# A two-layer graph network on one core: node projection from a transposed copy of x, later zeros, and an output bias added in two parts

## The reference

```python
# layer 0: attention over heads, one gathered row per node
xt = (x @ weight).reshape(-1, 4, 64)
alpha = softmax(leaky_relu((xt[src] * attn_l).sum(-1) + (xt[dst] * attn_r).sum(-1), 0.01), axis=1)
tmp = einsum('nh,nhd->nd', alpha[:n], xt[dst[:n]])
x = layernorm(x + tile(tmp over 4 heads))
# layer 1: messages over the 200000 edges
x_norm = layernorm(x) * ln_g + ln_b
q, k, v = x_norm @ Wq.T + bq, x_norm @ Wk.T + bk, x_norm @ Wv.T + bv
dk, dv = silu(edge_attr @ Wdk.T + bdk), silu(edge_attr @ Wdv.T + bdv)
attn = silu(sum(q[dst] * k[src] * dk, axis=1)) * cosine_cutoff(edge_weight)
agg = segment_sum(v[src] * dv * attn[:, None], dst)
x = layernorm(x + (x + agg @ Wo.T + bo))
```

## Time and profile before

| | |
|---|---|
| median of 3 runs | 3229.85 us (3221.85 to 3238.96) |
| profiled execution, its own time | 3223.67 us |
| its span | 3221.9 us |
| mean granted TensorE clock | 0.882 |
| TensorE / VectorE / ScalarE / GpSimd busy | 77% / 68% / 60% / 52% |
| bytes moved | 636.12 MB, mean 197 GB/s |

### The profile page before, as it was taken

The page is one execution under the profiler, slowest core; times in us unless marked ns, Lnnn a source line. Parts: engine busy times, 40 slices in busy tenths (PEclk is TensorE's granted clock), DMA queues, the critical chain, the costliest instruction groups (busy, mean ns, idle before and its releaser), DMA issues. The chain is left out here.

```text
span 3221.9 us, 50519 instructions
## 1 busy us (share of the span) xinstructions
PE 2495.6 (77%) x12110; PEld 2040.1 (63%) x12110; DVE 2182.9 (68%) x6172; ACT 1935.1 (60%) x4100; POOL 1667.0 (52%) x1791
## 2 busy tenths in 40 slices
PE   7287678887878787877888787888778787777776
PEld 5154566666666666666666666666666666666665
DVE  4276566776767676676776676777676776676668
ACT  4266466666666666566666666666666666665655
POOL 1554555555555555555555555555555555555533
PEclk9699888888899899889888899888888988888888
DMA  9464666766667676666666767676666766666653
GB/s 287 66 183 174 196 197 200 211 200 199 208 201 212 201 209 202 199 204 196 204 202 194 204 203 213 200 214 204 201 204 204 217 193 208 203 203 197 199 148 139
DMA packets 319094, 636.12 MB, mean 197 GB/s; under 512 B 83484, under 2 KB 140944, under 8 KB 319064
## 3 DMA queue, kind: packets, MB, share of 16 engines
q0 software_dynamic: 129840, 418.60, 45.0%
q1 hardware_dynamic: 188232, 214.41, 22.0%
q10 hardware_dynamic: 992, 2.79, 0.3%
HBM read 576.86 MB, written 58.74 MB: 197 GB/s over the span
## 5 line engine op out<-in xcount | busy, mean ns | idle before, releaser
L946 POOL DMA_INDIRECT e_kv<-kv_tab,e_idx x1568 | 1493.9, 953 | 1291.2 <-DVE e_gated L1146 684.2
L1074 ACT ACTIVATE e_gate_ps<-e_gate_ps 128x1024 f32<-128x1024 f32 x786 | 794.5, 1011 | 821.0 <-remote 441.5
L1146 DVE TENSOR_TENSOR e_gated<-e_kv,e_gate_ps 128x1024 f32<-128x1024 f32 x788 | 957.3, 1215 | 193.9 <-ACT e_gate_ps L1074 121.6
L1006 PE MATMUL e_gate_ps<-wd_hi_lo,high 128*128 128x512 f32 x1572 | 796.4, 507 | 247.6 <-DVE e_gated L1146 232.3
L1156 DVE CUSTOM_DVE_ANT_0 e_gated<-e_gated,e_q_ps 128x256 f32<-128x256 f32 x1576 | 593.8, 412 | 541.9 <-DMA q_tab<-l_q_out 225.0
L994 PE MATMUL e_sum_ps<-e_gated,weighed_hot 128*128 128x256 f32 x3168 | 908.6, 413 | 52.4 <-ACT weighed_hot L1090 30.4
L994 PEld LDWEIGHTS e_sum_ps<-e_gated,weighed_hot 128*128 128x128 f32 x3168 | 634.2, 211 | 155.1 <-ACT weighed_hot L1090 34.1
L1007 PE MATMUL e_gate_ps<-wd_bias,low 128*128 128x512 f32 x1572 | 666.1, 424 | 0.0
L1025 PE MATMUL e_q_ps<-q_win,hot_t 128*128 128x256 f32 x1572 | 467.3, 321 | 172.8 <-issue 114.1
L1006 PEld LDWEIGHTS e_gate_ps<-wd_hi_lo,high 128*128 128x128 f32 x1572 | 329.7, 210 | 332.5 <-DVE e_gated L1146 254.4
L1090 ACT ACTIVATE weighed_hot<-hot,e_attn 128x128 f32<-128x128 bf16 x1580 | 514.7, 399 | 32.2 <-DVE e_attn L1166 32.2
(11 more groups left out here) (157 smaller groups left out, 1469.3 us busy)
## 6 DMA issues: line engine op xcount, KB each, us to landing
e_attr<-attr_groups_dram SPq DMA_DIRECT2D x784, 128.0 KB
e_kv<-kv_tab,e_idx POOLq DMA_INDIRECT x1568
e_q_next<-q_tab SPq DMA_DIRECT2D x98, 256.0 KB
sum_tab<-e_sums SPq DMA_DIRECT2D x100, 128.0 KB
e_prior<-sum_tab SPq DMA_DIRECT2D x99, 128.0 KB
kv_tab<-l_kv_out SPq DMA_DIRECT2D x49, 256.0 KB
q_tab<-l_q_out SPq DMA_DIRECT2D x49, 256.0 KB
sum_tab<-zeros SPq DMA_DIRECT2D x10, 640.0 KB
```

Of the source, the lines that this page charges most:

```text
L946: pool.indirect_dma_start(kv[:, k, :], None, kv_tab, bass.IndirectOffsetOnAxis(ap=idx[:, k:k + 1], axis=0)).then_inc(kv_landed[k // G][k % ...
L1006: nc.tensor.matmul(gate_ps[:, k, :], high[:, s % 2, cols], wd_hi_lo[:], start=True, stop=False)
L1074: nc.scalar.activation(gate_ps[:, 2 * p:2 * p + 2, :], gate_ps[:, 2 * p:2 * p + 2, :], ACT.Silu).then_inc(silu_ready[s][p], 1)
L1146: nc.vector.tensor_tensor(gated[:, pair(s, p), :], kv[:, pair(s, p), :], gate_ps[:, 2 * p:2 * p + 2, :], ALU.mult).then_inc(gated_ready[s] ...
```

## The change

- TensorE no longer transposes x for the projection. A transposed copy of x (`x_turned`, prepared with the inputs) is loaded straight into `x_t`, which now holds all tiles; the transposes, their PSUM tile and ScalarE's copies are gone, and `xt_ps` has six slots for three.
- All of the first stage's loads but GpSimd's are issued by SyncE, the weights first. `bias_products` comes after tile 16. `round_and_sine` is split, the sine comes at tile 44.
- VectorE's six zeroed tiles come before the destination work; two multiplies and two reductions do what four and four did.
- x itself is loaded at the start of layer 0, by 14 DMAs, and VectorE waits for each chunk's part of it. The zeros of `sum_tab` are written in layer 0 too, 256 KB after each of the last 25 tiles.
- GpSimd adds the half bias to tiles 0 to 19 in layer 0, two after each of the last ten normalizations; to the other 29 in the output stage, each once TensorE has turned one more tile.
- In the output stage ScalarE takes the root of variance + eps, and VectorE the reciprocal of it. VectorE's `tensor_scalar` at L1375 is gone.

```diff
+BIASED = 20
...
+            SLOTS = 6
+            x_t = sb("x_t", [P, 2, TILES * P], F32)
...
+                        sp.dma_start(x_t[:, :, first:end], x_turned[:, first:end].rearrange("(k p) n -> p k n", p=P)).then_inc(landed[i], 16)
...
-                        if i % 2 and i // 2 < len(blank):
-                            rows = blank[i // 2]
-                            sp.dma_start(sum_tab[rows[0] * P:(rows[-1] + 1) * P, :].rearrange("(i p) c -> p i c", p=P),
-                                         zeros[:, 0:H].unsqueeze(1).broadcast_to([P, len(rows), H])).then_inc(zeroed, 16)
...
-                            pe.wait_ge(turned_copied, t - 1)
-                        for k in range(2):
-                            last = nc.tensor.transpose(turned_ps[:, t % 2, k * P:(k + 1) * P], x_sb[:, t, k * P:(k + 1) * P], ident[:])
...
-                            last = nc.tensor.matmul(xt_ps[:, t % SLOTS, 0:TAB], x_t[:, t % SLOTS, k * P:(k + 1) * P], w_ext[:, k, :], start=(k == 0), stop=(k == 1))
+                            last = nc.tensor.matmul(xt_ps[:, t % SLOTS, 0:TAB], x_t[:, k, t * P:(t + 1) * P], w_ext[:, k, :], start=(k == 0), stop=(k == 1))
                         last.then_inc(projected, 1)
-                        if t == 8:
+                        if t == 16:
                             bias_products()
...
+        zeroed = sem("zeroed")
+        blank = [range(a, min(a + 2, TILES + 1)) for a in range(0, TILES + 1, 2)]
...
+                        if t >= TILES - BIASED // 2:
+                            first = 2 * (t - TILES + BIASED // 2)
+                            pool.wait_ge(x1_ready, first + 2)
+                            for u in (first, first + 1):
+                                nc.gpsimd.tensor_tensor(x_sb[:, u, :], x_sb[:, u, :], bo_half[:], ALU.add).then_inc(biased, 1)
...
+                for g in range(CHUNKS):
+                    whole = [t for t in chunk(g) if (t + 1) * P <= x.shape[0]]
+                    if whole:
+                        sp.dma_start(x_sb[:, whole[0]:whole[-1] + 1, :],
+                                     x[whole[0] * P:(whole[-1] + 1) * P, :].rearrange("(i p) c -> p i c", p=P)).then_inc(x_landed[g], 16)
...
+                    if t + len(blank) >= TILES:
+                        part = blank[t + len(blank) - TILES]
+                        sp.dma_start(sum_tab[part[0] * P:(part[-1] + 1) * P, :].rearrange("(i p) c -> p i c", p=P),
+                                     zeros[:, 0:H].unsqueeze(1).broadcast_to([P, len(part), H])).then_inc(zeroed, 16)
...
+                            if i == 3:
+                                dve.wait_ge(x_landed[g], 16 * x_loads(g))
...
-                for t in range(COUNT):
+                for t in range(BIASED, COUNT):
+                    pool.wait_ge(turned, t - BIASED + 1)
                     nc.gpsimd.tensor_tensor(x_sb[:, t, :], x_sb[:, t, :], bo_half[:], ALU.add).then_inc(rest_ready, 1)
...
-                    act.wait_ge(inverse_ready, g + 1)
-                    nc.scalar.activation(rstd[:, span(chunks[g])], inverse[:, span(chunks[g])], ACT.Sqrt).then_inc(rstd_ready, 1)
+                    act.wait_ge(var_ready, g + 1)
+                    nc.scalar.activation(spread_of[:, span(chunks[g])], mean_var[:, span(chunks[g]), 1], ACT.Sqrt, bias=eps[:]).then_inc(root_ready, 1)
...
-                def invert(g):
-                    cols = span(chunks[g])
-                    dve.wait_ge(var_ready, g + 1)
-                    nc.vector.tensor_scalar(padded_var[:, cols], mean_var[:, cols, 1], EPS, None, ALU.add).then_inc(padded, 1)
-                    dve.wait_ge(padded, g + 1)
-                    nc.vector.reciprocal(inverse[:, cols], padded_var[:, cols]).then_inc(inverse_ready, 1)
...
                 def shifts(g):
                     cols = span(chunks[g])
+                    dve.wait_ge(root_ready, g + 1)
+                    nc.vector.reciprocal(rstd[:, cols], spread_of[:, cols]).then_inc(rstd_ready, 1)
```

More of the change, by code:

```diff
@@ L83, in gnn_kernel @@
         total = keep("total", [P, 1], I32)
+        zeros = keep("zeros", [P, 2 * H], F32)
         wd_hi_lo = keep("wd_hi_lo", [P, 2 * H], F32R)
@@ L152, in gnn_kernel @@
             angle_ready, sine_ready, bd_zero = sem("angle_ready"), sem("sine_ready"), sem("bd_zero")
-            landed = [sem(f"landed{i}") for i in range(len(pieces) + 1)]
+            landed = [sem(f"landed{i}") for i in range(len(pieces))]
             PAIRS = range(0, TILES, 2)
             LOTS = LOT // 2
-            blank = [range(a, min(a + 5, TILES + 1)) for a in range(0, TILES + 1, 5)]
-            assert len(blank) <= len(PAIRS) // 2
             stored = [sem(f"stored{j}") for j in range(LOTS)]
-            turned, turned_copied, projected, projected_copied = (
-                sem(n) for n in ("turned", "turned_copied", "projected", "projected_copied"))
+            projected, projected_copied = sem("projected"), sem("projected_copied")
             with nc.Block() as block:
@@ L167, in load @@
                         part = pieces[i]
-                        sp.dma_start(x_sb[:, part[0]:part[-1] + 1, :],
-                                     x[part[0] * P:(part[-1] + 1) * P, :].rearrange("(i p) c -> p i c", p=P)).then_inc(landed[i], 16)
-                    load(0)
+                        first, end = part[0] * P, min((part[-1] + 1) * P, N)
+                        sp.dma_start(x_t[:, :, first:end], x_turned[:, first:end].rearrange("(k p) n -> p k n", p=P)).then_inc(landed[i], 16)
                     sp.dma_start(w_ext[:, :, 0:H], weight.rearrange("(k p) n -> p k n", p=P)).then_inc(w_landed, 16)
@@ L382, in _ @@
                     dve.wait_ge(sine_ready, 1)
-                    then(nc.vector.tensor_scalar(phase[:], phase[:], -0.5, 0.5, ALU.mult, ALU.add))
-                    nc.vector.tensor_tensor(cut[:], cut[:], phase[:], ALU.mult)
-                    for t in (hot, weighed_hot):
-                        nc.vector.memset(t[:], 0.0)
-                    for t in (high, hot_t, q_win):
-                        nc.vector.memset(t[:].bitcast(F32), 0.0)
-                    nc.vector.memset(low[:].bitcast(F32), 0.0).then_inc(low_zero, 1)
-                    dve.wait_ge(low_zero, 1)
-                    for row in (64, 96):
-                        nc.vector.memset(low[row:row + 1, :, :].bitcast(F32), 1.0)
+                    then(nc.vector.tensor_scalar(dist[:], dist[:], -0.5, 0.5, ALU.mult, ALU.add))
+                    nc.vector.tensor_tensor(cut[:], cut[:], dist[:], ALU.mult)
         layer0(nc, dict(
-            x_sb=x_sb, ident=ident, wqkv=wqkv, first_idx=first_idx,
-            xt_tab=xt_tab, left_tab=left_tab, q_tab=q_tab, kv_tab=kv_tab, TILES=TILES, TAB=TAB))
+            x=x, x_sb=x_sb, ident=ident, wqkv=wqkv, bo_half=bo_half, first_idx=first_idx,
+            xt_tab=xt_tab, left_tab=left_tab, q_tab=q_tab, kv_tab=kv_tab, sum_tab=sum_tab, zeros=zeros, TILES=TILES, TAB=TAB))
         edge_stage(nc, dict(
@@ L425, in layer0 @@
 def layer0(nc, shared):
-    x_sb, ident, wqkv, first_idx = (shared[n] for n in ("x_sb", "ident", "wqkv", "first_idx"))
-    xt_tab, left_tab, q_tab, kv_tab, TILES, TAB = (shared[n] for n in ("xt_tab", "left_tab", "q_tab", "kv_tab", "TILES", "TAB"))
+    x, x_sb, ident, wqkv, bo_half, first_idx = (shared[n] for n in ("x", "x_sb", "ident", "wqkv", "bo_half", "first_idx"))
+    xt_tab, left_tab, q_tab, kv_tab, sum_tab, zeros, TILES, TAB = (
+        shared[n] for n in ("xt_tab", "left_tab", "q_tab", "kv_tab", "sum_tab", "zeros", "TILES", "TAB"))
     C = 5
@@ L497, in rows, with x_loads @@
             return slice(t * P, (t + 1) * P)
+        zeroed = sem("zeroed")
+        blank = [range(a, min(a + 2, TILES + 1)) for a in range(0, TILES + 1, 2)]
+        def x_loads(g):
+            return len({(t + 1) * P <= x.shape[0] for t in chunk(g)})
         with nc.Block() as block:
@@ L1262, in output_stage @@
         mean_var = sb("mean_var", [P, COUNT, 2], F32)
[L1263 to L1264 removed]
+        eps = sb("eps", [P, 1], F32)
+        spread_of = sb("spread_of", [P, COUNT], F32)
         rstd = sb("rstd", [P, COUNT], F32)
@@ L1400, in _ @@
                 gather_stats(last, chunks[last][-1])
-                invert(last)
                 shifts(last)
```

123 lines of the change are left out of this document (59 added, 64 removed).

## The result

The changed kernel takes 3206.14 us, median of 20 runs (3165.52 to 3227.0); the kernel before, in the same comparison, 3232.06. The ratio is 0.9898, interval 0.9869 to 0.9928; the ratio of the two medians is 0.9920. The ratio and its interval leave out as slow six of the changed kernel's 20 runs, those above 3213 us, and of the kernel before only one of 12596.77 us, so they lean towards a larger gain than the medians of all runs show. The change is faster either way, by 26 us by the medians and 23 to 42 by the interval. The forecast was 3196, range 3176 to 3216: the median lies inside it, 10 us above the forecast. The profiled execution took 3194.41 us, its span is 3192.3.

A forecast was written before the change was run, and what follows sets the result against it. Each stage has its own limit: DMA for the projection, TensorE for layer 0's second part, a held VectorE instruction in the output. Terms -19.6 - 13.5 + 1 + 2.5 = -29.6 gave 3194.1 or 3200.3; forecast 3196, range 3176 to 3216.

The forecast's parts named there:

- Output, -19.6: Output stage: the VectorE instruction held by GpSimd's unbroken adds and TensorE's slow restart go, -19.6 us, bounds -20 and 0.
- rows 7: Profile rows, layer 0's second part: VectorE's 0.17 us instruction amid 37 waited normalizations, read as showing an unbroken row holds.
- Projection, -13.5: Projection: transposes, copies and zeros go, tiles step 0.89 us, last copy at 70.0 instead of 83.34; bounds -23 and 0.
- Layer 0's first part, +1: Layer 0 start: 6.4 MB of x loads beside the gathers find room in the DMA engines, +1 us, bounds -5 and +47.
- Rival D: Layer 0's first part: x loads stop the gathers, then a backlog follows, +47 us, total 3242; chance 0.05.
- Layer 0's second part, +2.5: Layer 0's second part: last zeros land late, +1 us, and two adds delay a VectorE step, +1.5; bounds 0 and +15.
- Edges, 0: Edge stage, 2823.4 us, 88% of the span: the change doesn't touch it, so no difference.
- A: Rival, layer 0: all 20 GpSimd adds hold VectorE, 13.7 us in place of 1.5, total 3208; chance 0.12.
- B: Rival, output stage: the reciprocal is held until the adds end, so no gain there, total 3216; chance 0.06.
- C: Rival, projection: no gain, as loads land later or TensorE stays at the lower clock, priced at 3210; chance 0.09.
- E: Rival, more gain: projection follows the DMAs' bound, -23, or layer 0's first part loses steps, total 3185; chance 0.10.

The follow-up runs named there:

- e2: Kernel before, output stage's TENSOR_SCALAR removed (root first, then reciprocal), the 49 adds still in one row without waits: 3230.57 us, ratio 0.9997 to the kernel before.
- e8: Kernel before, only each of its 49 output-stage adds released by its turned tile: 2523.44 us, against 2544.33 for the kernel before on that chip, ratio 0.9913.
- e5: Changed kernel unedited, profiled a second time on the chip where the kernel before takes 2544.33 us: 2518.36 us, ratio 0.9892 to the kernel before.
- e7: Changed kernel with all 49 bias adds in the output stage, none in layer 0: 2508.97 us, against 2544.33 for the kernel before there, ratio 0.9862.
- e3: Changed kernel with the output stage of before and no adds in layer 0: 3224.38 us, ratio 0.9996 to the kernel before.
- e9: Changed kernel with GpSimd's backlog of normalizations in layer 0 released in fours: 3252.17 us, ratio 0.9905 to the kernel before.
- e10: Changed kernel with layer 0's normalizations released in fours and all 49 adds in the output stage: 3253.13 us, ratio 0.9925 to the kernel before.
- e12: Changed kernel with normalizations in fours and all 49 adds in the output stage, repeated on another chip: 3250.01 us, ratio 0.9922 to the kernel before.

## Why the prediction came out right, and where it did not

**Output, -19.6: measured -18.7.** The term is right, and so is the reason that carried it, GpSimd's unbroken row; I had also written that the gain comes "because the instruction is gone". e2 shows that half to be worth nothing and e8 that the release in step, with its gaps, is worth all. The Trainium skill, "SBUF — State Buffer", section "Who interferes with whom", has the kinds right: an instruction with two inputs in SBUF or a `tensor_scalar` can be held, the reciprocal with one input isn't. It has the wait end with one GpSimd instruction; here it lasted 19.36 and 17.58 us, to the end of the row, and 13.13 us, through some 24 instructions.

**Why rows 7 misled me.** From VectorE's short instructions in the middle of 37 normalizations I concluded that a wait in front of each keeps VectorE free. e5 has the same row, the same waits, and a hold of 13.1 us. A wait that is already met is no gap. Nor did the rows show that gaps kept VectorE free: the row of before has none where those instructions stand (248.93 to 256.64). What made the conclusion come out right for the output stage is that there, in step with TensorE, real gaps of 0.35 us stand between the adds. Why the normalizations hold VectorE on B and not on the slower chips is open.

**Projection, -13.5: measured -11.4.** The steps held: first landing 36.0 (35.71), bias products with the lower clock 2.7 + 1.5 (4.20), 0.89 for each copy, last copy 70.0 (70.78). From 83.34 to 70.0 is 13.3, not 13.5. The rest of the miss lies behind the last copy: from the last copy to the first gather 6.2 us went by before and 7.3 after. The sine at tile 44 pushes three copies together (69.13 to 70.3), so their stores leave together at the end; that this is the 1.1 us is likely, and no run has the sine elsewhere.

**Layer 0's first part, +1: measured -3.2** (first gather to the fourth chunk's scores, 68.8 for 71.9). The x loads did delay the chunks: first scores 11.7 us after the first gather (7.9 before), and the third alpha 61.7 after it (39.5 before). In the end it cost nothing there: the fourth alpha comes at 72 to 76 in every profile of the slower kind without pauses in the gathers, however early the third was. On B, where there is no standstill to hide in, the fourth alpha comes 3.9 us later in the changed kernel (e5, 42.9) than with the first stages of before (e8, 39.0), and the sixth 0.5 us earlier; without adds all of layer 0 is 1.0 us shorter (e7 against e8). So the delay was about 4 us, not 1, where it can be seen, and it was made up for later. The -3.2 on the slower chip lies inside the bounds (-5), and comes with a shorter standstill, 34 us for 46. Rival D was far off: GpSimd kept its 1.25 us a gather outside its pauses.

**Layer 0's second part, +2.5: measured +14.2.** This step failed in the profile after, in two parts. The adds cost 2.4 us, not 1.5 (measured on B). Some 7 us are the standstill between fourth and fifth chunk, which the four other profiles with these first stages and unpaced gathers on chips A, C and D (e3, e9, e10, e12) do not have at that place (13.8 to 15.2 us from alpha to alpha). The rest, some 5 us over eight chunks, I can't assign. On the slower chips those four take 226.0 to 229.1 us for layer 0, and the three profiles with the first stages of before 225.3 to 229.1. Of the four only e9 has the adds, so this says that the first stages' edit adds nothing to layer 0 in the mean, and that the profile after is the odd one.

**Edges, 0: measured -10.4.** Nothing in the runs ties this to the change: on chip A alone the same code took 2808.3 to 2840.7 us.

**Rivals.** A: the adds cost 2.4 us, not 13.7, and no VectorE instruction was held by them. B: nothing was held; in e2 it is the shift and not the reciprocal, and only without the gaps. C: the projection's gain was there on every chip. D did not happen. Of E the projection's -23 did not come, and a shorter first part did, by 3.2 us.

## What to carry over

A row of GpSimd instructions that runs without a real gap can hold a small VectorE instruction to its end, as in all three profiles of the output stage with one row of adds (19.36, 17.58 and 18.94 us) and in none of the other eleven. Look for VectorE instructions of a few columns that last over 2 us, and release each GpSimd instruction at the pace of its consumer; a wait that is already met is not enough, nor does it put a pause into a row of gathers. An edit that only delays work is to be priced where there is nothing for it to win (20.9 us on B). Where an untouched stage varies by more than the change is worth, cut both executions at marks that the change doesn't move and compare stages, and take a second profile before a loss of a few microseconds is given a cause.

## What the runs showed of the hardware

Chips differ by more than a quarter on this kernel: 2544 us on B, 3232 to 3284 on the others, and nearly all of the difference is in the two stages that gather. The projection and the output stage take the same time everywhere (87.5 to 89.5 us to the first gather with the old projection, 77.5 to 80.3 with the new; 68.6 to 70.0 for the paced output stage). DMA strip of 2000 to 2050 us, in the edge stage, 1.25 us a digit, of the profile after:

```profile
DMA  6568669767769800059898567668978767988898
```

and of the same kernel on B (e5):

```profile
DMA  9899999579999987788999987678999877799999
```

In the first all 16 DMA engines stand for three digits, some 3.75 us, together; on B they never do in this stretch. The waits view of the edge stage puts it in numbers, before and after (columns: us in total, times, longest). On B the view has no such row.

```profile
ACT e_gate_ps L1074 <- remote: 441.5, 149, 8.1
```

```profile
ACT e_gate_ps L1075 <- remote: 418.0, 157, 7.4
```

The other thing is the grid of 1.40 us: in a standstill each VectorE instruction that waits for the one before it starts 1.40 us after it, 0.20 otherwise. What paces it is open.
